# A four-stage transformer block on one core: half of the copies of turned attention maps move from VectorE to ScalarE, and the order of all engines is written anew

## What is computed

```python
x = x + jnp.tanh(g_xattn[0]) * _L0_xattn_ref(_layernorm(x), ctx, ctx, mask)   # 16 heads of 8, masked softmax
x = x + jnp.tanh(g_ffn[0])   * _L0_ffn_ref(_layernorm(x))                     # mixture of 8 experts, top 2
x = x + jnp.tanh(g_xattn[1]) * _L1_xattn_ref(_layernorm(x), ctx, ctx, mask1)  # 16 heads of 8, masked softmax
x = x + jnp.tanh(g_ffn[1])   * _L1_ffn_ref(_layernorm(x))                     # switched attention, 16 heads of 64
x = x + jnp.tanh(g_xattn[2]) * _L2_xattn_ref(_layernorm(x), ctx, ctx)         # mLSTM, 4 heads
x = x + jnp.tanh(g_ffn[2])   * _L2_ffn_ref(_layernorm(x))                     # quantised conv feed-forward
x = x + jnp.tanh(g_xattn[3]) * _L3_xattn_ref(_layernorm(x), ctx, ctx)         # one wide head and a feed-forward
x = x + jnp.tanh(g_ffn[3])   * _L3_ffn_ref(_layernorm(x))                     # mixture of 16 experts, top 4
```

## Time and profile before

| | before |
|---|---|
| median of three runs | 2446.69 us |
| profiled execution: its own time | 2447.47 us |
| profiled execution: its span | 2445.4 us |
| TensorE matmul busy | 2223.2 us (91%) |
| VectorE busy | 1749.4 us (72%) |
| ScalarE busy | 1290.7 us (53%) |
| mean granted TensorE clock | 0.976 |

### The profile page before, as it was taken

One profiled execution on the slowest core, in us unless ns is written; L12 is line 12 of the kernel. 1 busy time (PEld: TensorE's weight loads), 2 busy tenths in 40 slices (PEclk: granted clock), 3 DMA queues, 4 the chain that ended last, 5 costly groups with the idle time before them and its releaser, 6 DMA issues.

```text
span 2445.4 us, 51545 instructions
## 1 busy us (share of the span) xinstructions
PE 2223.2 (91%) x19938; PEld 1612.2 (66%) x19938; DVE 1749.4 (72%) x5567; ACT 1290.7 (53%) x3714; POOL 141.2 (6%) x180
## 2 busy tenths in 40 slices
PE   7899989989899998999899988999889998899998
PEld 3668657676567765677666766667666676666766
DVE  6874787757877577774877758777587775877657
ACT  4366354664547545474444744547344473445734
POOL 0000100001000010000100010000110001100010
PEclk9999999999999899998999999999899998999989
DMA  4034000340004300042000520006100061000610
GB/s 172 1 88 104 9 14 1 96 96 10 14 1 113 79 9 14 1 122 70 9 14 1 129 63 9 14 1 147 45 18 6 2 156 36 20 3 13 151 29 5
DMA packets 312516, 115.52 MB, mean 47 GB/s; under 512 B 268752, under 2 KB 295376, under 8 KB 312016
## 3 DMA queue, kind: packets, MB, share of 16 engines
q1 hardware_dynamic: 312272, 112.23, 17.9%
HBM read 63.96 MB, written 48.23 MB: 46 GB/s over the span
## 4 chain that ended last, share of the span: by engine, by line
PE 49%; DVE 30%; ACT 8%; DMA 5%; issue 4%; POOL 3%; SPq 1%; DVEq 0%; ACTq 0%
PE banks L450 7%; PE banks L386 6%; PE banks L589 3%; PE banks L505 3%; ACT PP L862 3%; PE banks L616 3%; PE banks L383 2%; PE banks L336 2%; DVE nm L1202 2%; DVE qk L1283 2%; DMA mix_d<-gs 2%; PE banks L544 2%; PE banks L397 2%; PE banks L559 2%; POOL mv L1741 2%
## 5 line engine op out<-in xcount | busy, mean ns | idle before, releaser
L862 ACT ACTIVATE PP<-banks,nm 128x128 f32<-128x128 f32 x1568 | 443.7, 391 | 210.8 <-DVE nm L1202 120.5
L1202 DVE TENSOR_REDUCE nm<-banks 128x4 f32<-128x512 f32 (+1 forms) x400 | 261.3, 675 | 136.3 <-PE banks L386 100.7
L336 PE MATMUL banks<-identb 128*128 128x256 bf16 x1840 | 289.1, 277 | 16.4 <-ACT PP L1017 8.5
L450 PE MATMUL banks<-w_sb,PP 128*128 128x128 f32 x1536 | 247.8, 285 | 45.7 <-ACT PP L862 17.6
L450 PEld LDWEIGHTS banks<-w_sb,PP 128*128 128x128 f32 x1536 | 167.4, 142 | 122.9 <-issue 64.0
L336 PEld LDWEIGHTS banks<-identb 128*128 128x128 bf16 x1840 | 177.2, 101 | 106.6 <-issue 48.0
L1741 POOL TENSOR_TENSOR mv<-mv,half 128x2 f32<-128x2 f32 x160 | 113.0, 706 | 2135.0 <-DVE mv L1099 2135.0
L1245 DVE COPY PP<-banks 128x512 f32<-128x512 f32 x256 | 175.8, 689 | 61.1 <-PE banks L450 60.2
L505 PE MATMUL banks<-w_sb,qk 128*128 128x128 f32 x1280 | 180.6, 280 | 2.0 <-DVE qk L1346 1.3
L505 PEld LDWEIGHTS banks<-w_sb,qk 128*128 128x128 f32 x1280 | 164.7, 194 | 20.1 <-issue 11.4
L386 PE MATMUL banks<-qk,gs 32*128 32x512 f32 x512 | 147.5, 653 | 0.0
(11 more groups left out here) (283 smaller groups left out, 4267.4 us busy)
## 6 DMA issues: line engine op xcount, KB each, us to landing
va<-v_d SPq DMA_DIRECT2D x32, 512.0 KB, 3.8
o_d<-oa SPq DMA_DIRECT2D x64, 256.0 KB, 4.2
va<-o_d SPq DMA_DIRECT2D x32, 512.0 KB, 4.4
pv_d<-PP SPq DMA_DIRECT2D x32, 256.0 KB, 2.0
oa<-pv_d SPq DMA_DIRECT2D x32, 256.0 KB, 3.2
v_d<-PP SPq DMA_DIRECT2D x16, 512.0 KB, 4.0
v_d<-tmp SPq DMA_DIRECT2D x16, 512.0 KB, 4.4
w_sb<-weights SPq DMA_DIRECT2D x1, 5599.0 KB, 24.2
```

What stands on the lines that cost most here:

```text
L336: pe.matmul(bank(k, n)[:, cols(c, T)], identb[:, :], bc(identb[:, :], 1, G), start=True, stop=True, skip_group_check=True)
L450: e = pe.transpose(bank(k, 2)[:, cols(j)], P[k][:, 512 * (u % 2) + 128 * j:][:, 0:128], ident)
L862: e = act.activation(P[k][:, 512 * (u % 2) + 128 * j:][:, 0:128], bank_[:, cols(j)], ACT.Exp, bias=nm[k][:, m:m + 1])
L1202: e = dve.tensor_reduce(m, b3(scores[:, 0:maps * 128], maps), AX.X, ALU.max, negate=True)
```

## The change

A tuple `ACT_TURNED` names the units 0, 2, 4 and 6. In both small attentions ScalarE copies their turned maps, each directly behind its exponentials of the following odd unit in the lane's sequence; VectorE keeps the copies of units 1, 3, 5 and 7. The ten lists of `BEATS_*` are new, VectorE's two now each with an order of its own, and so is `SPARES`: its 101 numbers sum to 115 before and to 99 after. `TURN` and all other code is as before.

```diff
+ACT_TURNED = (0, 2, 4, 6)
...
 BEATS_PE = ((
-    -1250, -612, -326, -44, 358, 653, 679, 1059, 1283, 1395, 1454, 1561, 1923, 2116, 2199, 2211, 2316, 2889, 2917, 2958,
+    -2094, -918, -186, 22, 399, 623, 948, 1025, 1243, 1313, 1313, 1318, 2001, 3016, 3040, 3072, 3152, 3893, 4028, 4258,
...
 SPARES = (
-    3, 1, 0, 0, 1, 0, 0, 0, 0, 0, 0, 0, 0, 0, 0, 0, 0, 0, 0, 1, 7, 0, 8, 0, 3, 0, 0, 0, 0, 0, 0, 0, 0, 0, 0, 0, 4, 0, 0, 0,
+    0, 0, 0, 0, 0, 0, 0, 0, 1, 0, 1, 0, 0, 0, 0, 0, 0, 0, 0, 0, 0, 2, 1, 0, 3, 0, 0, 0, 0, 0, 0, 0, 5, 1, 0, 0, 1, 0, 0, 0,
...
@@ -892,6 +895,9 @@
                 if u < 8:
                     yield
                     act_map(act, k, i, 8 * s + u, u, bank(k, u % 2), HQ)
+                if u - 1 in ACT_TURNED:
+                    yield
+                    act_map_turned(act, k, i, 8 * s + u - 1, u - 1, HQ)
                 if u == 5:
                     yield
                     gather_out(0)
@@ -1238,6 +1244,8 @@
                 dve_max(dve, k, i, 8 * s + u, 4 * (u % 4), bank(k, u % 2), HQ, s == 0)
                 if u % 2:
                     for n in (u - 1, u):
+                        if n in ACT_TURNED:
+                            continue
                         yield
                         dve.wait_ge(pT_ps[k], pT_ps.n(i, 8 * s + n))
                         if n >= 2:
```

More of the change, by code:

```diff
@@ L38 @@
 BEATS_PE = ((
[11 rows of a table removed]
-), (
[11 rows of a table removed]
[11 rows of a table added]
+), (
[11 rows of a table added]
 ))
 BEATS_ACT = ((
[7 rows of a table removed]
-), (
[7 rows of a table removed]
[8 rows of a table added]
+), (
[8 rows of a table added]
 ))
 BEATS_DVE = ((
[10 rows of a table removed]
-), (
[10 rows of a table removed]
[10 rows of a table added]
+), (
[10 rows of a table added]
 ))
 BEATS_POOL = ((
-    47832, 55688, 59143, 64674, 67070, 70207, 71015, 77823, 79861, 83113, 84484,
+    -10251, -6594, -1142, 4455, 8226, 11902, 13450, 16266, 19536, 21186, 21709,
 ), (
-    48901, 58347, 63494, 64749, 70006, 73170, 76144, 78979, 81361, 86183, 87523,
+    -7895, -3301, 1486, 5376, 11593, 15479, 16229, 18701, 20954, 26081, 27726,
 ))
 BEATS_SP = ((
-    -242752, -242553, -242553, -238131, -238131, -237804, -237804, -237058, -236981, -233923, -230618, -221598, -219346,
-    -218796, -217615, -212325, -212215, -209270, -206607, -206485, -203699, -203699,
-), (
-    -235003, -231213, -230164, -229008, -229008, -228143, -225901, -221262, -221262, -221262, -221262, -218853, -213790,
-    -209157, -209065, -206564, -205345, -205168, -204765, -204680, -203168, -203066,
+    -12650, -12533, -12533, -12533, -11766, -10993, -10225, -9970, -9521, -8722, -7246, 7356, 8466, 11132, 11200, 11200,
+    11504, 14847, 17165, 17442, 22523, 23924,
+), (
+    -9378, -9378, -9378, -9378, -6292, -920, 1298, 6635, 6635, 6846, 6858, 11371, 11884, 15248, 15248, 17100, 17341, 18028,
+    20307, 21929, 23326, 27216,
 ))
 SPARES = (
[3 rows of a table removed]
[3 rows of a table added]
 )
```

## The result

The changed kernel takes 2391.41 us (median of four runs, 2379.36 to 2396.78) beside 2446.59 us for the kernel before (2446.47 to 2448.3): a ratio of 0.976, 95% interval 0.973 to 0.979. It is 55 us faster. The forecast was 2427, 0.8% faster. All ratios are of undisturbed runs, which leaves out one of e16's, at 2446.51 us, over 1.5% above that kernel's fastest.

What follows compares the result with a forecast made beforehand. TensorE was taken as the bound, VectorE second. Terms of -21.5 (copies off VectorE), +10 (copies on ScalarE) and -8 (spares) gave -19.5 us from 2446.7, about 2427 us; range 2385 to 2470, the forecast's own 2405 to 2441.

Steps and rivals of the forecast that it cites:

- What bounds the kernel: Whole kernel: the chain passes on TensorE for 49%, VectorE 30%, ScalarE 8%, so VectorE is the second bound.
- the first rival: Small attentions and spares: all 43 us of VectorE's copies and 28 us of spares come off; 2400 us, chance 0.13.
- Copies taken from VectorE, -21.5 us: Small attentions: 128 copies, 88 us of work, leave VectorE; half of their 43 us on the chain is gained.
- Copies added to ScalarE, +10 us: Small attentions: 77 us more ScalarE work; copies behind exponentials cost 19 us, halved because the other lane fills gaps.
- The sign that I had named: TensorE in the profile after: waits for ScalarE's copies over 30 us would speak for the third rival.
- The third rival: Small attentions: ScalarE's queue becomes the lane's chain, 0.6 us per exposed round; 2471 us with 90 exposed, chance 0.19.
- the 49 rounds: Small attentions: with more than 49 of 128 rounds exposed to ScalarE's copy, the change was to turn slower.
- 29.5 us: Whole kernel: the gains set against the exposed copies, 21.5 us from VectorE's copies and 8 from spares.
- Spares, -8 us: TensorE, whole kernel: 256 fewer spare matmuls at 0.11 us, 28 us, times their 0.28 share on the chain.
- Slower by the clock: TensorE, whole kernel: fewer spares lower the mean clock from 0.976 to 0.95, costing 31 us; 2458 us, chance 0.10.
- The new order of the rest, nothing: Switched attention and the stages behind it: single pieces shifted, no row to price them, so 0 us.

Runs made afterwards that it cites:

- e16: Changed kernel with the split in small attention 0 alone; small attention 1's even copies back on VectorE, placed early: 2433.53 us, ratio 0.991 to the kernel before.
- e1: Kernel before with the split alone, keeping its order and spares, ScalarE's copy right behind the odd unit's exponentials: 2453.92 us, ratio 1.004 to the kernel before.
- e11: Changed kernel without the split: new order and spares, even copies back on VectorE, placed early: 2493.4 us, ratio 1.018 to the kernel before.
- e12: Changed kernel with each of ScalarE's 128 new copies split into four pieces: 2409.69 us, ratio 0.983 to the kernel before.
- e4: Kernel before with only the spare numbers of after: 2460.16 us, ratio 1.004 to the kernel before.
- e7: Changed kernel with no spare matmuls at all: 2433.74 us, ratio 0.994 to the kernel before.
- e3: Changed kernel with the spare numbers of before: 2451.8 us, ratio 1.001 to the kernel before.
- e14: Changed kernel with the old spare numbers only behind small attention 1, new ones up to there: 2434.43 us, ratio 0.993 to the kernel before.
- e6: Changed kernel with old order and spares up to the end of small attention 1, new ones behind, split everywhere: 2438.41 us, ratio 0.997 to the kernel before.
- e5: Changed kernel with new order and spares only up to the end of small attention 1, old ones behind, split everywhere: 2404.02 us, ratio 0.984 to the kernel before.
- e8: The changed kernel run again unaltered: 2395.83 us, ratio 0.981 to the kernel before.
- e9: Kernel before with 24 spare matmuls ahead of TensorE's first work: 2446.23 us, ratio 0.998 to the kernel before.

## Why the prediction was right in its sign and wrong in its size

*What bounds the kernel.* TensorE, VectorE and the chain were read rightly. Two steps failed. The sum prices the split, the copies and the spares each by rows of the old order, and has no term for the new order inside the small attentions; and what shut such a term out is a bound: "TensorE fills 3.4 us of a 3.56 us round, and 128 rounds that each lose the 0.16 us between give 20 us and no more". It rests on three rounds of the earlier trace rows. Over the whole stages a round takes 4.60 and 4.38 us before, so the room was 64 x 1.20 + 64 x 0.98 = 140 us, not 20, and 6.6 us a turn of it were won. For this bound I had held the gain low and the first rival (2400) unlikely. The result lies beyond that rival's figure, within my range.

*Copies taken from VectorE, -21.5 us.* The work is as forecast: 128 x 0.689 us, busy time -83 for the -88. As a term of the sum it is wrong. In the old order it is worth nothing (e1), and in the new one the split is worth 98 us (e11), part of it by the clock. It has no price of its own. On the chain after, all 43 us of VectorE's copies are gone, as the first rival had it, and 37 us of maxima that no rival counted.

*Copies added to ScalarE, +10 us.* Mis-sized. A copy takes 0.61 to 0.62 us by the mean, near the forecast 0.60, and the 128 together 79 us. ScalarE's busy time still rose by only 59 for the 77: the busy time of its other instructions is the same (1236 and 1238 us), but a copy's record overlaps those beside it, by 53 us in all instead of 31. On the chain L872 holds 4.7 us a turn where I expected 1, 37 us in all; by e12's slope, 0.6 to 0.8 of 79 us would be 47 to 63, an estimate, as it assumes that the slope holds down to nothing. The sign that I had named, waits of TensorE for these copies over 30 us, came: 74.4 us for L872, where 24.6 were switched attention's before. The third rival's mechanism is thus real and past the 49 rounds from which I said that it decides: 37 / 0.6 = 62 rounds by the chain. It did not decide because what stood against it was not 29.5 us but the new order. Halving this cost "as the two lanes' rounds lie in each other's gaps" was the error: in the dense order the chain passes through ScalarE's copy in the rounds from 628 to 636 us, one after the other; in the two behind them, to 643 us, spares and the values stand there instead. In the rows of after, L872 comes behind the odd unit's exponentials, which end at 628.35 us, and starts at 628.62, when the transposes have ended; ScalarE stood idle for 0.28 us between. That agrees with the FIFO rule of the Trainium skill ("PSUM — Partial Sum Buffer", section "Engine vs sequencer instructions") as to the sequence, but what this copy waited for was TensorE, not its queue.

*Spares, -8 us.* The sign is right, which is luck, and the reason wrong. The 16 fewer are not what counts: the same numbers on the old order cost 0.4% (e4), and none at all costs 38 us (e7). What counts is the place. The old numbers on the new order cost 55 us (e3), some 36 of them behind the small attentions (e14), by their own time in one stage and by the clock in others.

*Slower by the clock.* "With 14% fewer spares such stretches may become more" is true of the mechanism, as e7 shows with 0.938, in line with the rule of "TensorE: Matmul & The Clock Gate" (section "What's actually happening") that I set beside it. For this change it went the other way: the changed kernel's runs have 0.976 to 0.981 as means of its three groups, the kernel before's beside them 0.969 to 0.972.

*The new order of the rest, nothing.* This term, for switched attention and behind, was small in fact: by itself it gives 0.3% with its spares (e6), and from e5 to the changed kernel 8 us. The gain came from what had no term. My priced parts were e1's and e4's, and they sum to a loss; the new order of the small attentions, together with the split, is the gain: from e1 (1.004) to e8 (0.981), 58 us, 50 of them in the part with the small attentions (e5, 0.984).

Right were the sign, the place (most of the gain is in the stages with copies) and the work moved. Open are the 2.1 us a turn of e14 in switched attention, and which of the new lists, TensorE's, ScalarE's or VectorE's, shortens the end of small attention 0.

## What to carry to other kernels

When an engine is relieved under an order written by hand, the order decides whether the relief is worth anything: price the pair, and try the work's new place with the old order and the new order without the new place before believing either. Take the room in a stage from its whole length over its rounds, with the entry and exit of each lane, and never from a few adjacent rounds. Filler work belongs to one order; when the order changes it has to be placed anew, and its price is read stage by stage from the clock and from its own time on the chain, not from its count. Compare stages turn by turn: where one length comes back exactly and another with a lower granted clock beside it, the order and the clock can be told apart.

## What was not expected of the hardware

The same code found the higher clock from about 21 us in one execution and from about 34 us in another (the changed kernel and e8), worth 4.4 us of the first stage. In e9 the clock had risen to 2.4 GHz by 9.5 us, behind 24 matmuls back to back, and was at 1.2 GHz again from 15 to 42 us. In ScalarE's copy, four pieces of 128x128 take 0.80 us where one of 128x512 takes 0.62; four exponentials of 128x128 take 1.14. And 1584 spare matmuls are worth 38 us here, though each needs some 0.11 us on the engine that bounds the kernel.
